# Two-layer decoder on one core: the experts' shares are broadcast by DMA and multiplied by GpSimd instead of being spread by TensorE and multiplied by VectorE

## What is computed

```python
scores = jax.nn.softmax(xt @ Wg.T, axis=-1)                      # (T, 16)
# two of four groups by their largest score, then the 4 best experts in them
combine = jnp.zeros((T, E)).at[jnp.arange(T)[:, None], topi].add(weights)
h = jax.nn.silu(einsum('td,eid->eti', xt, W1)) * einsum('td,eid->eti', xt, W3)
expert_out = einsum('eti,edi->etd', h, W2)
y = einsum('etd,te->td', expert_out, combine)
z = jax.nn.silu(xt @ Ws1.T) * (xt @ Ws3.T) @ Ws2.T
return (y + z)
```

## Time and profile before

| | us |
|---|---|
| median of 3 runs | 535.25 |
| lowest and highest | 533.11, 536.31 |
| the profiled execution | 534.2 |
| span of its instructions | 532.4 |
| TensorE busy / VectorE / ScalarE / GpSimd | 493.6 / 396.9 / 345.2 / 190.4 |

### The profile page before, as it was taken

How to read it: one execution, slowest core, us unless ns; L and a number is a source line. 1 busy time by engine, 2 the same in 40 slices (tenths; PEclk the granted TensorE clock), 3 DMA queues, 4 the chain that set the end, 5 groups by cost and what they waited for, 6 DMA issues and landing times.

```text
span 532.4 us, 11834 instructions
## 1 busy us (share of the span) xinstructions
PE 493.6 (93%) x4694; PEld 362.3 (68%) x4721; DVE 396.9 (75%) x917; ACT 345.2 (65%) x601; POOL 190.4 (36%) x288
## 2 busy tenths in 40 slices
PE   5869887899999999999999999999999999999985
PEld 3424533567778788877887878777777676678654
DVE  2787997879677988548996587644876568689984
ACT  5666744766676236894269845588535874976796
POOL 3129986741340150330004072613052221032562
PEclk9987999899999999999999999999999999999999
DMA  8502443220000001000000020200000300000001
GB/s 290 216 0 63 149 162 114 71 81 1 1 3 1 2 10 71 1 2 2 1 1 2 1 80 3 81 1 1 1 1 2 120 1 1 1 2 2 0 27 55
DMA packets 5943, 21.66 MB, mean 41 GB/s; under 512 B 896, under 2 KB 3072, under 8 KB 5120
## 3 DMA queue, kind: packets, MB, share of 16 engines
q1 hardware_dynamic: 5888, 20.91, 11.6%
HBM read 19.86 MB, written 1.05 MB: 39 GB/s over the span
## 4 chain that ended last, share of the span: by engine, by line
PE 67%; DVE 16%; ACT 9%; issue 4%; POOL 3%; DMA 1%; ACTq 0%; DVEq 0%; POOLq 0%
PE ps L1072 24%; PE ps L1106 15%; PE ps L820 4%; DVE nmx L2524 3%; PE ps L951 3%; PE ps L844 2%; PE ps L880 2%; PE ps L1082 2%; PE ps L928 2%; PE ps L875 2%; PE ps L798 2%; PE ps L970 1%; PE ps L931 1%; DVE hl L2642 1%; PE ps L1152 1%
## 5 line engine op out<-in xcount | busy, mean ns | idle before, releaser
L2631 DVE TENSOR_TENSOR hs<-hs,ps 128x512 f32<-128x512 f32 (+1 forms) x68 | 45.2, 668 | 40.0 <-PE ps L1072 27.3
L1952 ACT ACTIVATE hs<-ps 128x512 f32<-128x512 f32 (+1 forms) x68 | 39.4, 581 | 51.1 <-PE ps L1072 42.7
L2524 DVE TENSOR_REDUCE nmx<-ps 128x2 f32<-128x512 f32 (+1 forms) x96 | 60.4, 681 | 7.2 <-PE ps L880 7.1
L556 POOL TENSOR_TENSOR ve<-mv,half 128x2 f32<-128x2 f32 x24 | 7.7, 322 | 149.0 <-DVE mv L2418 149.0
L1106 PE MATMUL ps<-w2h,hh 128*128 128x256 f16 x200 | 54.7, 274 | 0.7 <-DVE hl L2642 0.5
L1106 PE MATMUL ps<-w2h,hl 128*128 128x256 f16 x200 | 54.6, 273 | 0.0
L1106 PE MATMUL ps<-w2l,hh 128*128 128x256 f16 x200 | 54.6, 273 | 0.0
L1959 ACT ACTIVATE hh<-hs 128x512 f16<-128x512 f32 (+1 forms) x52 | 31.5, 611 | 34.5 <-DVE hs L2637 23.3
L2642 DVE TENSOR_TENSOR hl<-hs,hh 128x512 f16<-128x512 f32 (+1 forms) x52 | 40.1, 779 | 8.9 <-ACT hh L1959 8.6
L1911 ACT ACTIVATE pk<-ps 128x512 f32<-128x512 f32 x64 | 34.6, 597 | 12.1 <-PE ps L931 9.6
L1072 PE MATMUL ps<-yah,w1h 128*128 128x256 f16 x200 | 38.4, 274 | 1.9 <-DVE hs L2631 1.9
(11 more groups left out here) (249 smaller groups left out, 1338.5 us busy)
## 6 DMA issues: line engine op xcount, KB each, us to landing
stage<-in_w SPq DMA_DIRECT2D x12, 800.0 KB, 4.3
tstage<-in_tern SPq DMA_DIRECT2D x4, 1024.0 KB, 4.9
cs<-in_ctxT SPq DMA_DIRECT2D x1, 1024.0 KB, 9.4
cd<-in_ctxT SPq DMA_DIRECT2D x1, 1024.0 KB, 4.8
out_x<-xs SPq DMA_DIRECT2D x4, 256.0 KB, 2.2
sels<-in_sel SPq DMA_DIRECT2D x1, 800.0 KB, 9.8
w0s<-in_w SPq DMA_DIRECT2D x1, 768.0 KB, 7.0
xs<-in_x SPq DMA_DIRECT2D x1, 768.0 KB, 8.2
```

Source lines behind the costliest of these rows:

```text
L1952: act.activation(hs[:, n % 3, 0:w], ps[:, gate_bank(n), 0:w], ACT.Silu).then_inc(e_sil.sem, 1)
L2524: dve.tensor_reduce(nmx[:, int(n % 3 > 0), first + par:first + 2 * heads:2], ps[:, max_bank(it, n) + par, :].rearrange("p (h k) -> p h k", ...
L2631: TT(hs[:, n % 3, 0:w], hs[:, n % 3, 0:w], ps[:, up_bank(n), 0:w], ALU.mult).then_inc(e_hb.sem, 1)
```

## The change

1. The inner rows are put in another order. Tile e of each batch (e = 0 to 15) holds 128 rows of expert e. The 48 remaining rows of every expert form 6 tiles in which row r * 16 + e belongs to expert e. The shared experts' rows come last. So pairs 0 to 7 of a batch have one expert for each tile, pairs 8 to 10 have the 16 experts repeated eight times, and pairs 11 and 12 need no share. 11 of 13 pairs are multiplied, 44 of 52.
2. `router_experts` writes the shares as 32-bit floats, repeated eight times over the 128 columns, so that the turned `cT` already is the factor of pairs 8 to 10. TensorE turns it in 32 bits.
3. SyncE writes the 16 rows of `cT` to memory (`shares_out`), waits for that, and reads two experts' rows for each pair back into all 128 partitions (`shares_in`, 256 KB, three buffers `shs`).
4. `times_share(n)` moves to GpSimd and now stands between `silu_of` and `times_up`: `hs` times the share. `times_up` on VectorE waits for it. `inner_high` waits for `times_up`.
5. `spread` and its 100 matmuls are gone, with `sels` and its load. `up(n)` now waits for `silu_of(n-1)` only.
6. All four lists stand in a new order. TensorE's list has 43 fillers of 512 columns between the first gate and the last one of the Mixture, which had none: 3 and 4 at pairs 1 and 2, 3 at pair 12, 3 at pair 31, and 30 between pairs 32 and 37. `gate(0)` stands behind `first_output(1)`, five fillers, `maxima_turned(2)` and `scores_exp(2, 0)`, where it had stood ahead of all of them.

```diff
-            sp.dma_start(sels[:, :], sel0).then_inc(d_sel.sem, 16)
...
+            def shares_out(b):
+                sp.wait_ge(cw_ok.sem, b + 1)
+                sp.dma_start(shares[b].rearrange("(e t) -> e t", e=E0), cT[0:E0, b % 2, :]).then_inc(d_shw.sem, 16)
+                sp.wait_ge(d_shw.sem, 16 * b + 16)
+            def shares_in(b, p):
+                u = SHARE_PAIRS * b + p
+                if u >= 3:
+                    sp.wait_ge(e_hc.sem, share_turn(MOE_PAIRS * ((u - 3) // SHARE_PAIRS) + (u - 3) % SHARE_PAIRS) + 1)
+                sp.dma_start(shs[:, u % 3, :], shares[b:b + 1, 2 * S * p:2 * S * (p + 1)].to_broadcast([P, 2 * S])).then_inc(
+                    d_sh[u % 3].sem, 16)
...
+            def times_share(n):
+                kind, b, p = pair_of(n)
+                g.wait_ge(e_sil.sem, n + 1)
+                mine = hs[:, n % 3, :].rearrange("p (k t) -> p k t", k=2)
+                if p < SHARE_PAIRS:
+                    u = SHARE_PAIRS * b + p
+                    g.wait_ge(d_sh[u % 3].sem, 16 * (u // 3) + 16)
+                    share = shs[:, u % 3, :].rearrange("p (k t) -> p k t", k=2)
+                else:
+                    g.wait_ge(cw_ok.sem, b + 1)
+                    share = cT[:, b % 2, None, :].to_broadcast([P, 2, S])
+                g.tensor_tensor(mine, mine, share, ALU.mult).then_inc(e_hc.sem, 1)
...
                 if kind == "moe":
                     if n:
-                        pe.wait_ge(e_hc.sem, n)
+                        pe.wait_ge(e_sil.sem, n)
                     first_product(n, 1, up_bank(n), e_b)
...
             def times_up(n):
-                dve.wait_ge(e_sil.sem, n + 1)
                 if n < ALL_MOE:
                     dve.wait_ge(e_b.sem, n + 1)
+                if n < ALL_MOE and n % MOE_PAIRS < MASKED_PAIRS:
+                    dve.wait_ge(e_hc.sem, share_turn(n) + 1)
+                else:
+                    dve.wait_ge(e_sil.sem, n + 1)
...
             project(0, 1)
-            awake(1, 20)
+            awake_first(1, 24)
             stack(0, 0)
...
             scores_max(2, 5)
-            awake(6, 3)
-            pe.wait_ge(mx_ok.sem, 33)
-            gate(0)
-            pe.wait_ge(mx_ok.sem, 34)
-            up(0)
-            router_turned(1)
-            first_output(1)
-            pe.wait_ge(cw_ok.sem, 1)
-            spread(0)
+            first_output(1)
+            awake(7, 5)
+            router_turned(1)
+            maxima_turned(2)
+            scores_exp(2, 0)
+            gate(0)
+            scores_exp(2, 1)
+            up(0)
+            up(1)
+            awake(0, 3)
```

1402 lines of the change are left out of this document (671 added, 731 removed).

## The result

| | before | after |
|---|---|---|
| median of the runs (lowest to highest) | 535.66 us (533.11 to 536.31, 4 runs) | 558.60 us (557.19 to 559.72, 4 runs) |
| after over before | | 1.0441, 95% interval 1.0413 to 1.0468 |
| span of the profiled execution | 532.4 us | 558.2 us (its own time 559.72, granted clock 0.984) |

The forecast was 531.4 us, range 523 to 541. The time is 27 us above it and outside the range.

The account below looks back on a forecast made before the run. It took TensorE's list to bound the Mixture's stretch. The terms -11.0 + 9.5 - 3.0 + 2.6 - 2.0 = -3.9 us turned the profiled 534.2 into 530.3, as a median 531.4 us, range 523 to 541.

Parts of the forecast that it names:

- Part 1: In the Mixture's full stretch, 100 selection matmuls leave TensorE's list at 0.11 us each: -11.0 us.
- Part 2: Inside the Mixture, 43 added fillers occupy TensorE for +9.5 us, of which 3.0 us cover waits it had anyway.
- Parts 3 and 4: Mixture's start: work moved behind an earlier exponent product, +2.6 us; up to the first gate: narrower fillers, better clock, -2.0.
- Part 5: In the Mixture, VectorE loses 52 products (34.5 us), GpSimd gains 44 (56 us); average slack 1.7 us a pair: 0.
- Part 6: Shares through memory take 4.4 to 7.9 us, hidden for batches 1 to 3, perhaps late for batch 0: 0, up to +3.
- Part 7: After the Mixture, the same work in slightly other order: 0, +-2 us.
- The second: Rival: GpSimd's multiply delays `times_up` and the next gate, 0.2 us on each of 44 pairs: 540.4 us, chance 0.22.
- waits for `times_up` over 8 us: Sign in the profile after that the forecast is wrong: TensorE's summed waits for `times_up`, pointing to the GpSimd multiply rival.
- TensorE still over 95% busy: Sign in the profile after that the forecast holds: TensorE's busy share in the Mixture.
- The first rival: In the Mixture, fillers stand only where TensorE waits anyway, about half of their 9.5 us displacing nothing: 526.6 us, chance 0.20.
- The third: Rival: the gain goes back at the start through late batch 0 shares and moved work: 536.8 us, chance 0.18.

Follow-up runs that it names:

- a_no_fillers: The changed kernel without the 43 fillers of 512 columns inside the Mixture: 558.5 us, ratio to before 1.0450.
- hybrid_old: The kernel before, selection products kept, with the changed kernel's lists up to the first exponent product of turn 2: 536.5 us, ratio 1.0055.
- old_vector: The kernel before's lists and order, shares by DMA, no selection products, multiply on VectorE behind `times_up`: 541.7 us, ratio 1.0129.
- a_light_ternary: The changed kernel with `ternary`'s sum over partitions replaced by a copy and only the last of three passes in its three later calls: 553.8 us, ratio 1.0378.
- old_order_no_reduce: The new mechanism in the order of before, multiply on GpSimd ahead of `times_up`, `ternary`'s sum over partitions replaced by a copy: 572.7 us, ratio 1.0723.
- old_order: The new mechanism, multiply on GpSimd ahead of `times_up`, with the lists in the order of the kernel before: 605.9 us, ratio 1.1361.

## Why the prediction was wrong

**Part 1, the spreads, -11.0.** The 0.11 us for each was right as TensorE's work (11.3 us less busy), and wrong as a gain: 5.8 us by the ratios. This list, 98% busy, didn't hand over all that was taken out of it; a quarter (by the traces) to a half (by the ratios) became idle time.

**Part 2, the fillers, +9.5 - 3.0.** Wrong by its whole size, 6.5. Measured 0 (a_no_fillers). The forecast named the argument against itself, "30 of them stand in six pairs, which tells that some chain is long there", and used it for the wrong conclusion. Here the fillers inside a dense stretch were the mark of a wait that somebody had to bridge. Read so, they announced the loss.

**Parts 3 and 4, the start, +2.6 - 2.0.** Together +0.6 forecast; hybrid_old took 2.4 us more in the traces and 0.55% (2.9 us) in the runs, so the mechanism was right and the size too small. The parts were right in kind: maxima earlier (114.41 against 120.8 for their turning; the first exponent product at 115.16 against 122.34, where 119.7 was forecast), pairs later. The changed kernel around 114 us, the shares' copy on ScalarE and TensorE's turning, exponents and first gate, and the first multiply on GpSimd:

```profile
113.89 0.38 ACT L1952 ACTIVATE cT<-ps 128x256 f32<-128x256 f32 x1 [0.21 <-PE ps L1104]
...
114.41 0.27 PE L984 MATMUL ps<-idb,mtok 128*128 128x128 bf16 x2 [0.56 <-ACT cT L1952]
115.16 0.23 PE L1013 MATMUL ps<-mT,selh 48*128 48x128 bf16 x2 [0.47 <-ACT mT L1927]
...
115.72 0.39 PE L1156 MATMUL ps<-yah,w1h 128*128 128x256 f16 x2
...
119.89 1.26 POOL L627 TENSOR_TENSOR hs<-hs,shs 128x512 f32<-128x512 f32 x1 [0.90 <-DMA shs<-shares]
```

The granted clock from 36 to 48 us rose from 0.57 to 0.73, not to full. The first gate came at 115.72, earlier than forecast.

**Part 5, VectorE and GpSimd, 0. The reasoning failed, and its number came near by luck.** It set a chain of 2.9 us against 4.6 us of other work for each pair, called the 1.7 us left the slack, and took 0. In the order of before that is wrong by 70 us: TensorE waited 58.6 us for `times_up`, and the kernel took 605.9 us. An average said nothing of the places where GpSimd is occupied. Half of the 70 us is a term which the trace of before showed and I did not read, the 13 us in which each `ternary` holds GpSimd beyond its busy time, and a good part of the rest the wait for the shares. In the changed kernel the multiply costs 2 us, not because of any slack but because all lists were laid out anew around it. Whether the 34.5 us that VectorE gives up are worth 0, as forecast, no run shows by itself. The two engines do hold each other up: the low half's mean rose from 779 to 861 ns, and a product of 0.69 us in old_vector took 2.37 when it started just behind a pass of 1.89 on GpSimd. The Trainium skill (SBUF — State Buffer, Who interferes with whom) has a VectorE operation with two inputs in SBUF and a GpSimd operation that reads SBUF exclude each other, and the 2.37 agree with it. The forecast left this out of its sum; the one wait of TensorE that it lengthens was 3.3 us shorter in a_light_ternary.

**The order inside the Mixture, put at nothing. This is the step that failed.** The sum priced the list changes at the start and after the Mixture, and of those inside it only the fillers, without a reason for leaving out the rest. Measured with nobody multiplying the new order costs 19 us, with VectorE 30, and of these 30 some 21 behind pair 26. By the traces TensorE, full in the order of before (59.12 of 60 us), has work for only 45.75 of 60 us there. The change avoids the 70 us of its own chain by an order that costs about 20.

**Part 6, the shares' way, 0 up to +3.** In the changed kernel right: the copy starts at 113.89, the first multiply at 119.89, and GpSimd waits 0.9 us. The fixed cost of about 2 us for a DMA that the prediction takes from the Trainium skill (DMA: Bandwidth & Descriptors, Anatomy of one DMA) was not there for the 16 KB, which landed in 1.4. The reason given was wrong for the old order: "for batches 1 to 3 the routing comes well before its pairs" is not so, `cT` of batch 3 was copied at 330.7 us and pair 39 had its Silu at 332.9. There the route costs 7.8 us with VectorE and, by the traces of old_order_no_reduce, some 19 with GpSimd.

**Part 7, after the Mixture, 0 +- 2.** 2.3 us by the table of pairs (23.5 to 25.8).

**The rivals.** The second had the right sign, and its mechanism is that of old_order, not of the changed kernel; its mark, waits for `times_up` over 8 us, stayed at 6.3. None of the marks that I named as proof of error would have caught this result; of the signs for the forecast "TensorE still over 95% busy" failed (92%). The first rival's premise was right and its time wrong, and its sum takes the covered time off twice (4.7 for 9.5, and again -3.0). The third had the start about right. The own range of 528 to 535 is narrower than the ends of parts 2 to 4, which give 524 to 541; the result lies outside both.

**What stays open.** Why no better order for pairs 26 to 40 exists, or whether one does, the runs don't say. They show that most of the cost lies there, that a lighter `ternary` takes 6 us off these pairs in the traces and 3.4 off the whole, that the multiply is some 2 us of the whole (7 at most by the intervals), and that no engine is full. One wait was followed to its place in VectorE's list; which of the four lists would have to change wasn't tried.

## What to carry to other kernels

Before an operation is moved to a slower engine inside a loop between engines, price it in the order that exists, by the waits it would make at each turn and by everything that stands in the new engine's list, and then ask what order would hide it and what that order costs. An average slack is not a hiding place. Fillers that a change adds inside a dense stretch may mark waits: ask what they bridge before counting them as an expense. And an experiment that brings nothing may be a gain and a loss, so look at both in its trace.

## What the runs showed of the hardware

The sum over the partitions on GpSimd costs far more than its row says: in the changed kernel 0.44 to 1.0 us busy, but 5.7 to 6.0 us without an instruction before it and 7.0 to 7.5 after it, in each of the four calls; an ordinary operation in its place takes this away and in the old order 34 us with it. The shares' way through memory, from the end of the copy to `cT` in SBUF to the first multiply that reads the broadcast, took 5.6 us in the changed kernel and 5.0 in old_vector, with 1.4 us for the 16 KB out and 3.2 for the 256 KB in (medians).
